# Order of TensorE's work in an attention step, row transfers spread over the steps, and two products that nothing reads

## What is computed

```python
x = x + tanh(g_xattn[0]) * L0_xattn(layernorm(x), ctx, Wq, Wkv, Wo)
x = x + tanh(g_ffn[0])   * L0_ffn(layernorm(x), gate_w, w1, w2)
x = x + tanh(g_xattn[1]) * L1_xattn(layernorm(x), ctx, ctx, Wq, bq, Wk, bk, Wv, bv, Wo, bo)
x = x + tanh(g_ffn[1])   * L1_ffn(layernorm(x), Wr, br, W1, b1, W2, b2, gamma, beta)
```

## Time and profile before

| | us |
|---|---|
| median of three runs | 573.4 (572.22 to 574.28) |
| the profiled execution | 571.19 |
| its span, first to last instruction | 569.4 |
| TensorE busy | 440.4 (77% of the span), mean granted clock 0.826 |
| DVE / ScalarE / GpSimd busy | 336.9 / 214.2 / 237.4 |
| row transfers L576 | 64 indirect DMAs |

### The profile page before, as it was taken

How to read it: one execution, slowest core, us unless ns; L and a number is a source line. 1 busy time by engine, 2 the same in 40 slices (tenths; PEclk the granted TensorE clock), 3 DMA queues, 4 the chain that set the end, 5 groups by cost and what they waited for, 6 DMA issues and landing times.

```text
span 569.4 us, 16851 instructions
## 1 busy us (share of the span) xinstructions
PE 440.4 (77%) x5346; PEld 334.9 (59%) x5350; DVE 336.9 (59%) x1255; ACT 214.2 (38%) x608; POOL 237.4 (42%) x378
## 2 busy tenths in 40 slices
PE   7788889878576899999478787877865799999300
PEld 4465455545444699998145555544544699999300
DVE  4678556755438656666338855754544756666493
ACT  4434323232232444442044432323221566666221
POOL 7023543453443144445102354435345244554456
PEclk9599785978855999999869968677875999999855
DMA  7791000000000122221200010000010122222241
GB/s 222 213 314 22 21 20 2 22 21 20 20 18 25 47 67 67 70 65 52 74 10 21 20 39 30 4 18 21 20 50 28 42 57 68 63 68 65 70 121 55
DMA packets 38672, 32.06 MB, mean 56 GB/s; under 512 B 6984, under 2 KB 32245, under 8 KB 38613
## 3 DMA queue, kind: packets, MB, share of 16 engines
q1 hardware_dynamic: 34069, 21.86, 14.0%
q0 software_dynamic: 4544, 9.41, 5.1%
HBM read 20.26 MB, written 10.99 MB: 55 GB/s over the span
## 4 chain that ended last, share of the span: by engine, by line
PE 53%; DVE 20%; issue 8%; another core or an unknown queue 8%; ACT 3%; POOL 3%; DMA 2%; DVEq 1%; POOLq 1%; ACTq 0%; SPq 0%
PE bank L671 49%; PE bank L674 4%; DVE room L1288 4%; DVE mx L1265 4%; ACT room L1052 2%; DVE room L1295 1%; DMA o_rows<-room,ids 1%; DVE v_s L1167 1%; POOL wa L648 1%; DVE x L1250 1%; DVE x L1302 1%; DVE wa L1497 1%; DVE fstats L1307 1%; DVE wa L1490 1%
## 5 line engine op out<-in xcount | busy, mean ns | idle before, releaser
L623 POOL DMA_INDIRECT o_rows<-room,ids x78 | 77.7, 996 | 101.0 <-DVE room L1438 37.2
L671 PE MATMUL bank<-room 128*128 128x128 f32 x624 | 83.8, 277 | 2.9 <-issue 2.0
L671 PE MATMUL bank<-wa,room 128*128 x624 | 83.0, 276 | 1.3 <-ACT room L1110 1.1
L671 PEld LDWEIGHTS bank<-room 128*128 128x128 f32 x624 | 75.7, 192 | 6.1 <-ACT room L1115 3.1
L671 PEld LDWEIGHTS bank<-wa,room 128*128 128x128 f32 x624 | 76.1, 192 | 2.0 <-issue 1.9
L576 POOL DMA_INDIRECT xg_rows<-xfa,slots x64 | 63.9, 998 | 32.0 <-issue 19.0
L1265 DVE TENSOR_REDUCE mx<-bank 128x4 f32<-128x324 f32 x128 | 54.4, 487 | 36.2 <-PE bank L671 36.2
L988 ACT ACTIVATE room<-bank 128x128 f32<-128x128 f32 (+1 forms) x110 | 31.2, 284 | 107.2 <-PE bank L674 104.7
L1288 DVE RECIPROCAL room<-bank 128x128 f32<-128x128 f32 x32 | 30.6, 956 | 60.6 <-remote 47.4
L1052 ACT ACTIVATE room<-bank 128x384 f32<-128x384 f32 x128 | 52.4, 495 | 27.0 <-PE bank L671 27.0
L1415 DVE COPY room<-wa 128x512 f32 x78 | 33.3, 427 | 39.2 <-issue 20.3
(11 more groups left out here) (191 smaller groups left out, 733.9 us busy)
## 6 DMA issues: line engine op xcount, KB each, us to landing
room<-xg_rows SPq DMA_DIRECT2D x78, 65.5 KB
wa<-in_L_ffn_w SPq DMA_DIRECT2D x1, 2048.0 KB, 10.1
wb<-in_L_ffn_W SPq DMA_DIRECT2D x1, 2048.0 KB, 17.1
ob<-o_rows SPq DMA_DIRECT2D x32, 64.0 KB, 1.9
wb<-o_rows SPq DMA_DIRECT2D x6, 256.0 KB, 4.5
o_rows<-room,ids POOLq DMA_INDIRECT x78
x<-in_x SPq DMA_DIRECT2D x4, 256.0 KB, 4.4
xg_rows<-xfa,slots POOLq DMA_INDIRECT x64
```

The lines of the kernel that those rows point to most:

```text
L623: pool.indirect_dma_start(out=o_dram[l], in_=o_sb[t.slot(UN)][:, :], in_offset=None, out_offset=bass.IndirectOffsetOnAxis(ap=ids[t.slot(UN ...
L671: return pe.matmul(out_, lhsT, rhs, start=start, stop=stop)
```

## The change

Four edits, all inside the attention stages.

1. *TensorE's order.* `turn_max` stands ahead of `scores`, and `less_max` right behind them. The turn of xn and wo come after it; then the logits, in layer 0 `more_values`, the turns of xfa. The rank products stay behind `weights`.
2. *Routing one step later.* `due` gives the pair that a step serves: the choice of experts reads pair s - 6 (`chosen`) instead of s - 5, placing reads pair s - 7 (`placed`) instead of s - 6; the last pair keeps its steps (s = 20 and s = 21). On DVE, ons follows the reciprocal at once, ranks and logits are read next, and the choice and the placing come at the end of a step. The pair's statistics are all made on the even step.
3. *Row transfers.* GpSimd issues two in every step, for one batch: the even batch of pair s - 8, the odd batch of pair s - 9. The pair 12, 13 goes with four in s = 20 behind the two of batch 11, the last pair with four in s = 21.
4. *Unread products.* Two bf16 products of 512 columns into bank 2 at the end of every step that has scores, which puts them ahead of the next step's products for the maxima.

```diff
+        def due(s, n, last):
+            if s.c == B - 1 + last:
+                return Step(B - 1)
+            return Step(s.c - n) if live_pair(s.back(n)) and s.c - n < B - 1 else None
+        def chosen(s):
+            return due(s, 6, 5)
+        def placed(s):
+            return due(s, 7, 6)
...
@@ GpSimd
-                    ready = b6 if b6.c == B - 1 else b7
-                    if live_pair(ready) and (ready.c == B - 1) == (ready is b6):
-                        S["f4"].wait(pool, ready)
-                        S["f2"].wait(pool, ready)
-                        scatter(ready, 0)
-                        scatter(ready, 1)
+                    for b, js in ((b8, (0,)), (b9, (1,))):
+                        if live_pair(b) and b.c < B - 3:
+                            S["f4"].wait(pool, b)
+                            S["f2"].wait(pool, b)
+                            for j in js:
+                                scatter(b, j)
+                    if s.c >= B + 4:
+                        b = placed(s)
+                        ...
+                        scatter(b, 0)
+                        scatter(b, 1)
...
@@ TensorE
-                    if live_pair(b5):
+                    if placed(s):
+                        ranks(placed(s), s)
+                    if live_pair(b5) and b5.c == B - 1:
                         logits(b5)
-                    if live_pair(b6):
-                        ...
-                    if l == 0:
-                        more_values(s)
                     if live(b2):
+                        turn_max(b2)
                         scores(b2)
-                        turn_max(b2)
+                        less_max(b2)
+                    if live(s):
+                        S["xn"].wait(pe, s)
+                        tr(bank[4][:, NC * T:NC * T + P], xn[s.slot(2)][:, :], P).then_inc(S["t1"].sem, 1)
                     if live(b3):
                         S["rc"].wait(pe, b3)
                         ...
-                    if live(b2):
-                        less_max(b2)
-                    if live(s):
-                        ...
+                    if live_pair(b5) and b5.c < B - 1:
+                        if placed(s):
+                            S["f4"].wait(pe, placed(s), 1)
+                        if l == 0:
+                            pe.wait_ge(v_kept, min(s.c + 1, B))
+                        logits(b5)
+                    if l == 0:
+                        more_values(s)
                     if live_pair(b4):
                         S["f2"].wait(pe, b4)
                         ...
+                    if live(b2):
+                        unread(bank[2][:, :], 2)
...
@@ DVE
                         dve.reciprocal(den[:, :], bank[6][:, T:2 * T]).then_inc(rc.sem, 1)
-                    if l == 0 and late_batch(s.c) is not None:
-                        ...
-                    if live(b3):
                         rc.wait(dve, b3, 1)
                         S["wo"].wait(dve, b3.back(1))
                         dve.tensor_tensor(ons[:, :], bank[6][:, 0:T], den[:, :], ALU.mult).then_inc(rc.sem, 1)
+                    if placed(s):
+                        if chosen(s):
+                            S["lg"].wait(dve, chosen(s))
+                        read_ranks(placed(s))
+                    if chosen(s):
+                        read_logits(chosen(s))
+                    if l == 0 and late_batch(s.c - 1) is not None:
+                        ...
...
+                    if live_pair(b3):
+                        ...
                         for j in range(2):
+                            dve.bn_stats(fstats[:, j, :], x[:, seq(b3.back(1 - j))]).then_inc(f1.sem, 1)
                         for j in range(2):
+                            f1.wait(dve, b3, j + 1)
+                            dve.bn_aggr(fmv[:, j, :], fstats[:, j, :]).then_inc(f1.sem, 1)
+                    if placed(s):
+                        place(placed(s))
+                    if chosen(s):
+                        choose(chosen(s))
```

More of the change, by code:

```diff
@@ L864, in logits, with ranks @@
                     ins.then_inc(S["lg"].sem, 1)
+                def ranks(b, s):
+                    S["f3"].wait(pe, b, 8)
+                    S["cu"].wait(pe, b.back(2))
+                    if live_pair(s.back(5)):
+                        S["c2"].wait(pe, s.back(5))
+                    if l == 0 and b.c == 1:
+                        hear(pe, "consts")
+                    r0, r1 = bank[7][:, 272:280], bank[7][:, 280:288]
+                    mm(r0, tri[:, :], mb[:, 0, :], True, False)
+                    mm(r0, onesb[:, :], cum[:, :], False, True)
+                    mm(r1, tri[:, :], mb[:, 1, :], True, False)
+                    mm(r1, onesb[:, :], mb[:, 0, :], False, False)
+                    mm(r1, onesb[:, :], cum[:, :], False, True).then_inc(S["rk"].sem, 1)
                 def step(s):
-                    b1, b2, b3, b4, b5, b6 = (s.back(n) for n in (1, 2, 3, 4, 5, 6))
+                    b1, b2, b3, b4, b5 = (s.back(n) for n in (1, 2, 3, 4, 5))
                     if live(b2):
@@ new lines, in choose @@
+                def choose(b):
+                    f3, two = S["f3"], xfa[:, b.c - 1:b.c + 1, D + 1:D + 3]
+                    if l == 0 and b.c == 1:
+                        hear(dve, "consts")
+                    f3.wait(dve, b, 1)
+                    for j in range(2):
+                        dve.max(top[:, j, :], lg[:, j, :]).then_inc(f3.sem, 1)
+                    f3.wait(dve, b, 3)
+                    for j in range(2):
+                        dve.max_index(topi[:, j, :], top[:, j, :], lg[:, j, :]).then_inc(f3.sem, 1)
+                    f3.wait(dve, b, 5)
+                    dve.tensor_copy(two, topi[:, :, 0:2]).then_inc(f3.sem, 1)
+                    f3.wait(dve, b, 6)
+                    S["f4"].wait(dve, b.back(2))
+                    ohv = oh[:, :, :].rearrange("p (j k) e -> p j k e", k=2)
+                    dve.tensor_tensor(ohv, iota8[:, :].unsqueeze(1).unsqueeze(1).to_broadcast([P, 2, 2, E]),
+                                      two.unsqueeze(3).to_broadcast([P, 2, 2, E]), ALU.is_equal).then_inc(f3.sem, 1)
+                    f3.wait(dve, b, 7)
+                    S["cu"].wait(dve, b.back(2))
+                    dve.tensor_tensor(mb[:, :, :], ohv[:, :, 0, :], ohv[:, :, 1, :], ALU.add).then_inc(f3.sem, 1)
+                    dve.tensor_tensor(gap[:, b.c - 1:b.c + 1], top[:, :, 1], top[:, :, 0], ALU.subtract).then_inc(f3.sem, 1)
@@ new lines, in read_ranks, with place @@
+                def read_ranks(b):
+                    S["rk"].wait(dve, b)
+                    dve.tensor_tensor(rk[:, :, :], bank[7][:, 272:288].rearrange("p (j e) -> p j e", j=2),
+                                      bc3(regoff[:, :], 2), ALU.add).then_inc(S["f4"].sem, 1)
+                def place(b):
+                    f4, c = S["f4"], b.c
+                    f4.wait(dve, b, 1)
+                    dve.tensor_tensor(pick[:, :, :].rearrange("p (j k) e -> p k j e", k=2),
+                                      oh[:, :, :].rearrange("p (j k) e -> p k j e", k=2),
+                                      rk[:, :, :].unsqueeze(1).to_broadcast([P, 2, 2, E]), ALU.mult)\
+                        .then_inc(f4.sem, 1)
+                    f4.wait(dve, b, 2)
+                    with nc.allow_low_precision(reason="row numbers, exact in float32 and int32"):
+                        dve.tensor_reduce(slots[:, c - 1:c + 1, :].rearrange("p j k -> p (j k)"), pick[:, :, :],
+                                          AX.X, ALU.add).then_inc(f4.sem, 1)
```

98 lines of the change are left out of this document (29 added, 69 removed).

## The result

The changed kernel takes 518.6 us (median of four runs, 516.58 to 521.27) where the one before takes 573.2: a ratio of 0.905, with a 95% interval of 0.900 to 0.910. The profiled execution took 521.27 us, its span is 519.3, TensorE's mean granted clock 0.873 (before 0.826). The forecast was 542, the range 514 to 580: right in sign and inside the range, but the gain is 54.6 us where 31 were forecast. In all that follows, medians are over every run, and ratios leave out the three runs (two of the change timed again, one with the unread products in layer 1 only) that lay over 1.5% above the fastest of their kernel.

What follows compares the result with a forecast made beforehand. Attention steps were taken as bound by the hold of four row transfers and the clock fall behind it. Profiled 571.2 − 30.7 (18 steps) − 0.5 (tails) = 540.0; the runs' median lies 2.2 higher, so 542 us, range 514 to 580.

Steps and rivals of the forecast that it cites:

- The path and the hold: Attention steps: turn after mxp, scores, less_max, exponentials; two transfers hold TensorE's hand-overs for up to 3.35 us from the first.
- step at full clock: Attention steps with routing: 7.15 us, the middle between 6.4 without a hold and 7.9 with all of it.
- The base step: Attention step with all its work, full clock, no hold: bound by DVE at 6.4 us.
- The hold of a pair: Two transfers per step hold the residual add; between nothing and 1.5 us per step, the middle taken.
- The clock: Steps 8 to 17: a quarter of the time at the lower level, 9.9 us there; mean 7.8, −30.7 us over 18 steps.
- The order and the later routing: Attention steps: turned order worth little once routing runs; POOL's cum and the scatter simply follow one step later.
- The beginnings: Early steps: steps 4 to 7 gain 0.2 to 0.4 us each, each layer's first two pay 0.97 each; sum 0.
- The tails: Layer ends: s = 18 gives −2.5 us per layer, s = 20 costs +2.5 and +2.0; together −0.5.
- B: Attention steps: a pair makes no hold, DVE's 6.4 us decides; −55.9 us, 517 us with the tails; chance 0.17.
- C: Attention steps: hold paid once per group, a second tail; mean step 9.4 us, −2.0, 571 us; chance 0.18.
- D: Attention steps: clock never recovers, all 18 steps cost 10.9 us; +25.1, 598 us; chance 0.15.

Runs made afterwards that it cites:

- O + S: The changed kernel without its two unread products per step (new order, later routing, two transfers in every step): 519.8 us, ratio 0.899 to the kernel before.
- O alone: Kernel before with only the new TensorE order and routing a step later; four transfers in every second step, no unread products: 533.1 us, ratio 0.931.
- the repeated run: The changed kernel, unchanged, timed again in five rounds beside the same without unread products: 519.7 us, ratio 0.902 to the kernel before.
- first comparison: First timings of the changed kernel with and without its two unread products per step: 518.6 and 519.8 us, ratios 0.905 and 0.899 to the kernel before.

## Why the prediction was right in sign and 23 us short

*The path and the hold: right.* mxp, the turn, less_max and the exponentials follow each other as forecast; the reciprocal lost its idle time; a pair makes a partial hold in each step. The forecast's step at full clock, 7.15 us, is near the 6.99 measured, by two errors that nearly cancel, which is luck. **The base step** was put at 6.4 for every step, bound by DVE. Without a hold it is 6.0: DVE does work without a gap, but that is 6.3 us only in the step with the choice (326.90 − 320.69 and 339.09 − 332.82 give 6.2 and 6.3) and 5.9 in the step with the placing. I had the load of the fuller step in both. **The hold of a pair** was put at 0.75 in each of 18 steps; it costs 1.1 for each of 16 pairs, 1.0 per step. It was also put in the wrong place: over the residual add, with an end 1.95 us behind the second start. It falls on the exponentials first, and ends for them 2.1 us behind the first start.

*The clock: the step that failed.* I took a quarter of the time at the lower level, with steps of 9.9 us, because holds come twice as often (16 pairs against ten groups, in fact). That term was 0.69 us per step, 12.4 of the 14.6 us by which the 18 steps came out lower. The granted clock was 0.97 and 1.00. A hold of 2 us beside which TensorE still has the turn of xn, wo, logits or turns, and the unread products, leaves it idle for some 1.3 us ahead of the next products; the earlier trace rows had already shown that the fall followed 1.65 us of work in 3.6. I had written that down in the forecast and then weighed the count of holds, not their depth. The price was off too. Without the unread products (O + S) the clock is 0.92 and 0.90, so 16 and 20% of the time at the lower level, not far from my quarter; yet the steps take 6.95 and 7.26 us, where my 7.8 would be 7.6 without those products. Against the 6.96 and 7.02 of the change, where the clock is 0.97 and 1.00, the lower clock cost nothing in layer 0 and 0.24 us per step in layer 1.

*The order and the later routing: mis-sized.* "Worth little once routing runs" and "simply follow one step later" were not both right. O alone took 38 us from the 18 steps (9.51 to 7.40 us), more than any other part, though one group of four per layer left the stretch by it (eight groups in 18 steps, before ten). I had counted what the order saves in a quiet step, and not that the routing one step later moves the group within the step: the reciprocal is now in front of it and less_max at its beginning, so that the 4 us of the earlier trace rows mostly fall away even with four transfers. How much of the 38 us is the order and how much the later routing stays open, since no run has one without the other. Since the change has all, this did not spoil the sum, but it gave the credit to the split and the clock.

*The beginnings: missed, −8.3 us.* s = 3 to 8 gained 3.7 and 6.8. In layer 1 the five steps take 5.35 to 5.68 us; before, three of them took 6.14 to 6.23, the first 8.29 at a clock of 0.66 and the last 7.56. The forecast had worked out 5.5 from the exponentials and then replaced it by 6.0 for TensorE's sum; the sum of work behind less_max was too high for steps without routing. That explains 1.8 of the 6.8 us. The first step gave 2.9, with the clock at 0.99, and varies (6.39 us in the execution of the repeated run); the last gave 2.0, where DVE is busy 5.1 us instead of 6.6, the choice of experts being a step later. Of the +2.2 at the start of layer 0 1.6 lie ahead of the first products for the maxima (19.35 against 17.74 us), and are no work of the change: the execution of the repeated run has 17.74 there again.

*The tails: missed by 3 us.* Forecast −0.5, measured +2.4 (0.8 in layer 0, 1.6 in layer 1). I took 2.5 us off in each layer because s = 18 has two transfers where four stood, and left out that s = 17 and s = 19, which had none, now have two each. From s = 17 to the first transfer of s = 20 layer 1 gained 0.6 us (20.4 to 19.8). The ten transfers that close the layer then take longer than the eight before. GpSimd's in layer 1, from the timeline, to be read with the earlier trace rows (first of s = 19, first of s = 20, last of s = 21):

```profile
378.74 1.09 POOL L588 DMA_INDIRECT xg_rows<-xfa,slots  x1 [0.18 <-issue]
...
382.19 0.98 POOL L588 DMA_INDIRECT xg_rows<-xfa,slots  x1 [0.51 <-DVE rk L1349]
...
394.60 1.24 POOL L588 DMA_INDIRECT xg_rows<-xfa,slots  x1 [0.30 <-issue]
```

From the first start of s = 20 to the last of s = 21 it is 12.4 us, before 9.7: +2.7, inside the 2.5 to 4.4 allowed. But 2.5 of it were taken as slack, and the way from the last transfer to the first tile load gave back only 0.5 us (4.6 to 4.1).

*The rivals.* B's number, 517, was hit by a mechanism that is not B's: the pair holds in every step. By the numbers alone one would have drawn the wrong lesson, and only the kernel without transfers in the steps tells it. C wanted the second tail in full; cutting a group does add one (the pairs have holds of their own, 16 in the place of ten), but it falls where only 1.1 us of it is on the path. The Trainium skill, "DMA: Bandwidth & Descriptors", states in its section on the anatomy of a DMA that the fixed cost of a GpSimd transfer is about 2.0 us; the 2.07 to 2.18 us from a first start to the exponentials are near it, but they time the release of another engine's work and not a landing, other releases came at 3.63 and 5.82, the rule says nothing of what else stands still meanwhile, and the time did not come out as C made it. D fell outright: the clock was 0.97 and 1.00 where D needs less than 0.75.

## What to carry to other kernels

When GpSimd's indirect transfers hold the hand-overs from TensorE, look where in the step the group begins: here a hand-over given at its very start mostly passed at about 2 us, and one given 1.6 us later could wait for the whole group, with exceptions that stayed unexplained. Place the long waits' cause against the path first, then split it evenly, and only then fill TensorE; each of the three alone recovered a part of the same loss (7, 6 and 2%), together 9.5%. When an edit that moves work to another step goes with an edit of the order, time them apart: here they were not, and the largest part has two owners. And a number that lands on a rival is no proof of it: measure the step without the cost before saying that the cost is nothing.

## What the runs showed of the hardware that was not expected

- The hold has a time inside the group: releases at 2.1 us and at 5.8 to 5.9 us behind the first of four starts, by when TensorE's products were issued (less_max 0.3 us behind it; the weights until 1.6, less_max at 2.4). A pair can also let a hand-over pass without delay: less_max at 0.91 to 1.30 us in the kernel with the split alone, the exponentials 0.43 to 0.59 us behind it.
- Pairs of transfers cost the path 1.0 us per step (7.0 against 6.0 us; 1.1 us a pair), and not the 2.1 us of their hold; both kernels that moved pairs ahead in the step were slower.
- Unread products raised the mean granted clock from 0.77 to 0.85 in the kernel before (2.3% faster), and from 0.92 and 0.90 to 0.97 and 1.00 in the changed one (first comparison), without a gain that could be measured there. Beside O with groups of four they did not raise it (0.92 and 0.90 without, 0.90 and 0.88 with them).
